# A gated feed-forward stage in seven block products instead of eight, joined on VectorE, and a new order in the openings of the conv phases

## What is computed

```python
def _L3_ffn_ref(x, U1, V1, U2, V2, b1, b2):   # HIDDEN 1024, INTER 2752, RANK 256
    P = jnp.einsum('bsh,hr->bsr', x, U1)
    H = jnp.einsum('bsr,rf->bsf', P, V1) + b1
    gate, up = (H[..., :INTER], H[..., INTER:])
    act = jax.nn.silu(gate) * up
    Z = jnp.einsum('bsi,ir->bsr', act, U2)
    out = jnp.einsum('bsr,rh->bsh', Z, V2) + b2
    return out
...
x = x + _L3_ffn_ref(_L3_cond_ref(x, cond_512, ...), L3_ffn_U1, L3_ffn_V1, L3_ffn_U2, L3_ffn_V2, L3_ffn_b1, L3_ffn_b2)
```

## Time and profile before

| | |
|---|---|
| median of 3 runs | 2100.54 us (2098.27 to 2106.67) |
| the profiled execution | 2105.4 us, its span 2103.2 us |
| mean granted clock of TensorE | 0.98 |
| busy in the span: TensorE, VectorE | 1970.7 us (94%), 1291.9 us (61%) |
| busy in the span: ScalarE, GpSimd | 961.5 us (46%), 368.6 us (18%) |
| the gated stage | from about 1688 us to the end |

### The profile page before, as it was taken

How to read it: one execution, slowest core, us unless ns; L and a number is a source line. 1 busy time by engine, 2 the same in 40 slices (tenths; PEclk the granted TensorE clock), 3 DMA queues, 4 the chain that set the end, 5 groups by cost and what they waited for, 6 DMA issues and landing times. The chain is left out here.

```text
span 2103.2 us, 32178 instructions
## 1 busy us (share of the span) xinstructions
PE 1970.7 (94%) x10213; PEld 1667.7 (79%) x10213; DVE 1291.9 (61%) x2326; ACT 961.5 (46%) x1547; POOL 368.6 (18%) x457
## 2 busy tenths in 40 slices
PE   4799968899999979998899999988999999999999
PEld 4688834799999868886788878877888878878886
DVE  6888888877767763327667676656555443344333
ACT  4488744555555421114344444424666544433442
POOL 4122212111111100002111111112121222222221
PEclk9899999999999999999999999999999999999999
DMA  7567547321121154444221112223333211142114
GB/s 189 175 194 198 175 166 244 94 67 60 60 89 61 51 188 150 136 133 147 72 71 60 51 55 64 66 65 120 101 100 110 82 54 45 52 140 88 49 45 164
DMA packets 118608, 222.30 MB, mean 106 GB/s; under 512 B 18336, under 2 KB 65184, under 8 KB 117792
## 3 DMA queue, kind: packets, MB, share of 16 engines
q1 hardware_dynamic: 102048, 212.36, 32.2%
q10 hardware_dynamic: 16512, 9.31, 1.6%
HBM read 159.04 MB, written 62.59 MB: 105 GB/s over the span
## 5 line engine op out<-in xcount | busy, mean ns | idle before, releaser
L2666 DVE SCALAR_TENSOR_TENSOR f_prod<-ps,b,f_gate 128x512 f32<-128x512 f32 (+1 forms) x88 | 66.0, 751 | 170.9 <-ACT f_gate L2606 170.9
L125 POOL TENSOR_TENSOR rows<-l_EY,ones 128x4 f32<-128x4 f32 x128 | 31.1, 243 | 740.0 <-ACT rows L1346 380.4
L2707 POOL TENSOR_TENSOR x_lo<-f_prod,x_hi 128x512 fp32r<-128x512 f32 (+1 forms) x88 | 105.0, 1193 | 288.2 <-ACT x_hi L2613 288.2
L2536 PE MATMUL ps<-pt_hi,v_hi 128*128 128x512 f32 (+1 forms) x352 | 138.0, 392 | 1.7 <-PEq L637 1.7
L2536 PE MATMUL ps<-pt_lo,v_hi 128*128 128x512 f32 (+1 forms) x352 | 137.8, 391 | 0.0
L2536 PE MATMUL ps<-pt_hi,v_lo 128*128 128x512 f32 (+1 forms) x352 | 137.2, 390 | 0.0
L2606 ACT ACTIVATE f_gate<-ps,b 128x512 f32<-128x512 f32 (+1 forms) x88 | 60.6, 689 | 157.8 <-PE ps L2536 157.7
L1085 PE MATMUL ps<-l_u_hi,l_g_hi 128*128 128x512 f32 x272 | 113.6, 418 | 5.7 <-DVE l_g_lo L1606 3.6
L1572 DVE SCALAR_TENSOR_TENSOR rows<-ps,dem3e,l_middle 128x512 f32<-128x512 f32 x60 | 45.1, 752 | 119.5 <-ACT l_middle L1315 97.4
L125 POOL TENSOR_TENSOR XE<-rows,ones 128x8 f32 (+1 forms) x96 | 21.1, 243 | 536.4 <-DVE rows L1782 260.8
L1085 PE MATMUL ps<-l_u_lo,l_g_hi 128*128 128x512 f32 x272 | 110.3, 406 | 0.0
(11 more groups left out here) (407 smaller groups left out, 5802.1 us busy)
## 6 DMA issues: line engine op xcount, KB each, us to landing
x<-rows SPq DMA_DIRECT2D x64, 512.0 KB, 2.9
xin<-x SPq DMA_DIRECT2D x96, 256.0 KB, 4.0
rows<-x SPq DMA_DIRECT2D x48, 512.0 KB, 4.1
out<-rows SPq DMA_DIRECT2D x32, 512.0 KB, 2.6
v<-in_ffn_v SPq DMA_DIRECT2D x84, 128.0 KB, 2.6
xin<-in_x SPq DMA_DIRECT2D x16, 512.0 KB, 5.8
xb<-in_x SPq DMA_DIRECT2D x16, 512.0 KB, 3.3
x<-xb SPq DMA_DIRECT2D x16, 512.0 KB, 2.6
```

The lines of the kernel that those rows point to most:

```text
L2536: mm = nc.tensor.matmul(ps[0:m, 2 * g + gu, :], v1sp[ws][:, s, r, gu, 0:m], pt[ms][:, r, cols], start=(k == 0), stop=(k == 5))
L2666: v.scalar_tensor_tensor(prod[0:m, g, :], ps[0:m, 2 * g + 1, :], b1[0:m, 1, bass.ds(2 * i + g, 1)], gate[0:m, g, :], ALU.add, ALU.mult).th ...
L2707: nc.gpsimd.tensor_tensor(asp[1][0:m, g, :], prod[0:m, g, :], asp[0][0:m, g, :].bitcast(F32), ALU.subtract).then_inc(al_ready, 1)
```

## The change

In the gated stage all blocks but n = 0 and n = 22 use a scheme of seven block products. The four outputs (gate and up, each for the two g) are a 2x2 product of weights (rank group r by gate or up) and tokens (r by g), which takes eight products of 128x128 by 128x512. The scheme takes seven, of mixed weights and mixed tokens, and adds products up afterwards:

- Weights: four mixes of the V1 block (additions and subtractions of 128x128, `mix_v1`), split like V1 itself (128x512, lines 2658 and 2800). One own quarter isn't used as such, so the own split has 384 columns.
- Tokens: at the start of each half `raw_tokens` adds high and low part again (128x2048), `mix_tokens` makes four mixes (128x512), and their high and low parts follow as 128x2048. The second half's stand between its first half's output additions.
- Products: seven of three matmuls each. Products 1 and 4 add up in bank 0, 2, 5 and 6 in bank 1, 3 and 7 in bank 2 or 3.
- Joins on VectorE (`join`, line 2814), 128x512 each, a bank plus an SBUF tile: `second` = bank 1 + `first`; `part` = bank 1 + `first`; `part` += bank 2 or 3; `first` += bank 1; `second` += bank 2 or 3. `first` is ScalarE's copy of bank 0 after product 1 (`read_first`, 2700). The gate for g = 0 is read out of bank 0, the gate for g = 1 out of `second`, up for the two out of `first` and `part`, all three in SBUF.
- V2 is split in two halves, in blocks 1 and 20, instead of at the start.
- ScalarE splits the U2 block n at the start of block n instead of at the end of block n-1, and copies bank 0 ahead of the high part of g = 1's product.

In the openings `edges_p` waits for the split low part of u instead of `g_summed` and writes banks 7 and 1; a group of four filling matmuls becomes one of two; ScalarE does `cross_g(0)` ahead of chunks that stood before it, and `split_h(0)` ahead of one; VectorE does `split_h(0)` ahead of a chunk; GpSimd's chunks wait for the low part of g.

```diff
             def edges_p():
                 pe.wait_ge(ue_ready, n)
-                pe.wait_ge(g_summed, g0 + 1)
+                pe.wait_ge(ul_ready, 2 * g0 + 2)
...
                     edges_p()
                     if layer > 0:
-                        K.turn_over(nc, ps, 7, 4)
+                        K.turn_over(nc, ps, 4, 2)
                     main(0)
...
+            if len(chunks) > 0:
+                pool.wait_ge(gl_ready, g0 + 1)
             for k in range(min(POOL_CHUNKS, len(chunks))):
                 chunk(k)
...
+                def seven(i, n, s, short, half=half):
...
+                    pe.wait_ge(w_lo, 2 * n + 1)
+                    pe.wait_ge(silu_ready, 2 * n - 1)
+                    product(0, m, own(1, 0), tokens(1, 0), True)
+                    if isinstance(n, int) and n == half * NIB + 1:
+                        pe.wait_ge(prod_ready, 2 * n)
+                        pe.wait_ge(mix_t_lo, used + half + 1)
+                    else:
+                        pe.wait_ge(joined, used + 5 * at - 1)
+                    product(1, m, mixed(2), mixed_tokens(0, 1), True)
+                    product(2 + s, m, mixed(0), mixed_tokens(1, 0), True)
+                    pe.wait_ge(first_ready, used + at + 1)
+                    product(0, m, own(0, 0), tokens(0, 0), False)
+                    pe.wait_ge(joined, used + 5 * at + 1)
+                    product(1, m, mixed(1), mixed_tokens(1, 1), False)
+                    project(i - 1, n - 1, 1 - s, 0, False)
+                    pe.wait_ge(joined, used + 5 * at + 2)
+                    product(1, m, own(0, 1), mixed_tokens(0, 0), False)
+                    pe.wait_ge(joined, used + 5 * at + 3)
+                    product(2 + s, m, mixed(3), tokens(0, 1), False)
+                    project(i - 1, n - 1, 1 - s, 1, False)
...
+            def read_first(n, m, half):
+                act.wait_ge(gu_done, products_before(n, half) + 1)
+                act.wait_ge(prod_ready, 2 * n - 1)
+                nc.scalar.activation(first[0:m, :], ps[0:m, 0, :], ACT.Copy).then_inc(first_ready, 1)
...
+            def join(n, half, k, out, src, bank, m):
+                product = (2, 5, 5, 6, 7)[k]
+                at = 5 * (n - half - 1)
+                dve.wait_ge(gu_done, products_before(n, half) + product)
+                if k == 0:
+                    dve.wait_ge(first_ready, used + n - half)
+                if k == 1:
+                    dve.wait_ge(prod_ready, 2 * n)
+                if k > 1:
+                    dve.wait_ge(joined, used + at + 2)
+                v.tensor_tensor(out[0:m, :], ps[0:m, bank, :], src[0:m, :], ALU.add).then_inc(joined, 1)
...
+                if is_whole(n):
+                    up = ps[0:m, 2 * g + 1, :]
+                else:
+                    dve.wait_ge(joined, used + 5 * (n - half - 1) + 4)
+                    up = (first, part)[g][0:m, :]
...
+                    join(n, half, 0, second, first, 1, m)
+                    split_u2(n, s, short)
+                    if not last and not is_whole(n + 1):
+                        mix_v1(n + 1, 1 - s, next_short, half)
+                    join(n, half, 1, part, first, 1, m)
+                    join(n, half, 2, part, part, 2 + s, m)
+                    if not last:
+                        split_v1(n + 1, 1 - s, next_short)
+                    join(n, half, 3, first, first, 1, m)
+                    multiply(i, n, 0, m, half)
+                    join(n, half, 4, second, second, 2 + s, m)
+                multiply(i, n, 1, m, half)
```

More of the change, by code:

```diff
@@ L1428, in first_pair @@
                 cross_g(1)
[L1429 to L1431 removed]
+                if layer == 0:
                     split_g(1)
                 split_h(0)
[L1434 to L1437 removed]
+                if layer > 0 and not fast:
+                    split_g(1)
                 some_chunks(len(chunks))
@@ L2468, in gated_ffn @@
         asp = [t[:, :, 0:HALF] for t in K.Xs]
+        part = sb("part", [P, HALF])
+        mix_w = sb("mix_w", [P, 4, P])
+        mix_wsp = [sb("mix_w_hi", [P, 2, 4, P], F32R), sb("mix_w_lo", [P, 2, 4, P], F32R)]
+        mix_t = K.c_raw[:, 0:2 * T].rearrange("p (r t) -> p r t", r=2)
+        mix_tsp = [t[:, 0:2 * T].rearrange("p (r t) -> p r t", r=2) for t in K.c_part]
+        first, second = K.xin[:, 0, :], K.xin[:, 1, :]
         zsp = [sb("z_hi", [P, 2, T], F32R), sb("z_lo", [P, 2, T], F32R)]
@@ L2479, in gated_ffn, with is_whole, products_before @@
         block = ctx.enter_context(nc.Block())
+        def is_whole(n):
+            return isinstance(n, int) and n % NIB == 0
+        def products_before(n, half):
+            return 7 * n - 5 * (half + (not is_whole(n)))
         def blocks(eng, half, body):
@@ L2539, in gate_up, with product @@
                     mm.then_inc(gu_done, 1)
-                def project(i, n, s, g, short):
-                    m = rows_of(short)
-                    pe.wait_ge(al_ready, 2 * n + g + 1)
-                    if g == 0:
-                        pe.wait_ge(w_lo, 2 * n + 2)
-                    start = isinstance(i, int) and i == 0
-                    if start and half == 1 and g == 0:
-                        pe.wait_ge(xo_ready, NT)
-                    for r in range(2):
+                def product(out, m, weights, moving, start):
+                    for k, (ws, ms) in enumerate(PASSES):
+                        mm = nc.tensor.matmul(ps[0:m, out, :], weights[ws], moving[ms],
+                                              start=(start and k == 0), stop=(k == 2), skip_group_check=True)
+                    mm.then_inc(gu_done, 1)
@@ new lines, in project @@
+                def project(i, n, s, g, short, ranks=(0, 1)):
+                    m = rows_of(short)
+                    start = isinstance(i, int) and i == 0
+                    if 0 in ranks:
+                        pe.wait_ge(al_ready, 2 * n + g + 1)
+                        if g == 0:
+                            pe.wait_ge(w_lo, 2 * n + 2)
+                        if start and half == 1 and g == 0:
+                            pe.wait_ge(xo_ready, NT)
+                    for r in ranks:
@@ L2588, in _, with split_v1 @@
         def _(act):
-            def split_v1(n, s, short):
+            def split_v1(n, s, short, half):
                 m = rows_of(short)
@@ L2620, in body @@
                 last = short and n == 2 * NIB - 1
-                silu(i, n, 0, m)
-                if not last:
-                    split_v1(n + 1, 1 - s, next_short)
-                act_hi(n, 0, m)
-                silu(i, n, 1, m)
-                act_hi(n, 1, m)
-                if not last:
-                    split_u2(n + 1, 1 - s, next_short)
+                after = half + (isinstance(i, int) and i == NIB - 1)
+                if is_whole(n):
+                    silu(i, n, 0, m, half)
+                    if n == 0:
+                        mix_tokens(0)
+                    else:
+                        split_u2(n, s, False)
+                    split_v1(n + 1, 1 - s, next_short, after)
+                else:
+                    split_u2(n, s, short)
+                    if not last:
+                        split_v1(n + 1, 1 - s, next_short, after)
+                    silu(i, n, 0, m, half)
+                act_hi(n, 0, m)
+                silu(i, n, 1, m, half)
+                if is_whole(n):
+                    act_hi(n, 1, m)
+                    if n > 0:
+                        mix_tokens(1)
+                if not short:
+                    read_first(n + 1, rows_of(next_short), half)
+                if not is_whole(n):
+                    act_hi(n, 1, m)
+                if isinstance(n, int) and n in (1, NIB - 2):
+                    split_v2(int(n > 1))
+            act.wait_ge(const_loaded, 32)
             for half in range(2):
-                blocks(act, half, body)
+                blocks(act, half, lambda i, n, s, first, short, half=half: body(i, n, s, short, half))
                 for g in range(2):
@@ new lines, in mix_tokens @@
+            def mix_tokens(half):
+                g0, g1 = slice(0, HALF), slice(HALF, T)
+                done = 5 * half
+                for k, (r, g, left, right) in enumerate((
+                        (1, g0, (1, g1), (1, g0)), (1, g1, (0, g1), (1, g1)),
+                        (0, g1, (0, g1), (1, g0)), (0, g0, (0, g0), (0, g1)))):
+                    dve.wait_ge(mix_t_ready, used + done + k + 1)
+                    v.tensor_tensor(mix_t[:, r, g], mix_t[:, left[0], left[1]], mix_t[:, right[0], right[1]],
+                                    ALU.subtract).then_inc(mix_t_ready, 1)
@@ L2660, in split_u2, with multiply @@
                                 ALU.subtract).then_inc(w_lo, 1)
-            def multiply(i, n, g, m):
+            def multiply(i, n, g, m, half):
                 dve.wait_ge(silu_ready, 2 * n + g + 1)
```

157 lines of the change are left out of this document (113 added, 44 removed).

## The result

The changed kernel took 2180.22 us (median of 4 runs, 2172.92 to 2187.27) against 2101.47 (4 runs): a ratio of 1.0377, 95% interval 1.0350 to 1.0405. A second set gave 2174.40 (5 runs), ratio 1.0348 (1.0308 to 1.0388). The forecast was 2162, range 2130 to 2190, slower with 0.90. The profiled execution took 2172.92 us, its span 2171.1.

What follows compares the result with a forecast made beforehand. TensorE's matmuls bound the gated stage before; VectorE's dependent chain would bound it after. Intervals +53.6, edges +6.1 + 3.4 + 0.7 + 3.0 - 4.4 + 4.5 and openings -5.5 gave +61.4, so 2162 us, range 2130 to 2190.

Steps and rivals of the forecast that it cites:

- The interval: Gated stage, block to block: VectorE's chain takes 9.62 us against 8.28 before, +53.6 us over 40 intervals.
- u_lo: VectorE's low part of U2 in each block: held by GpSimd's instruction, ending 2.12 us after the second multiply.
- Second product: VectorE's second multiply in each block: two SBUF operands, held by GpSimd, ending 0.61 us after it, at 9.62.
- TensorE stays the bound: Rival for the gated stage: VectorE's chain under 7.6 us, interval 7.58, time about 2080; chance 0.06.
- The edges: Gated stage outside steady intervals: start +6.1, V2 split +3.4, mixing +0.7, block 23's weights +3.0, first intervals -4.4, half ends +4.5.
- Start: Start of the gated stage: block 1 begins at 1699.8 against 1693.7 before, +6.1 us.
- end of the first half: Last projection of the half waits for VectorE, ScalarE and GpSimd: 2.25 us at each half's end, +4.5 for both.
- mixes of tokens and outputs: Second half's token mixing, placed between the first half's output additions: +0.7 us.
- the one on the clock: Rival for the gated stage: TensorE's stalls lower the clock, +4.6 us an interval, 2346 if throughout; chance 0.04.
- The split of V2: V2's split, moved in halves to blocks 1 and 20 behind the second multiply: 1.7 us each, +3.4.
- The openings: Openings of the four conv phases: edge product no longer waits for VectorE's sum; -5.5 us, between 0 and -14.
- No overlap of VectorE's instructions: Rival: each VectorE instruction starts only when the previous ends, 10.4 us a block, 2194; over 2190, this or register waits: 0.05.

Runs made afterwards that it cites:

- pool_short: Changed kernel with GpSimd's low part of the product cut from 512 to 16 columns a time: interval 8.63 us, gated stage 447.2 us.
- join4_early_pool_short: Changed kernel with join4 and second silu moved earlier and GpSimd's low part cut to 16 columns: 2099.86 us, ratio 0.9996 to before; interval 7.71.
- extra_add: Changed kernel with one more 128x512 VectorE addition and a wait in each of the 42 mixed blocks: interval 10.16 us, stage 512.4 us.
- filled: Changed kernel with unread filling matmuls in four of TensorE's pauses in the gated stage: stage 481.6 us, whole 2168.1 and 2168.3 us.
- after_again: The changed kernel unedited, run for a second trace: 2184.96 us, gated stage 488.1 us.
- join4_early: Changed kernel with join4 ahead of the first product on VectorE, second silu ahead of the first high part on ScalarE: 2139.13 us, ratio 1.0192 to before.

## Why the prediction came out as it did

**The interval: right, and its steps too.** Forecast 9.62, measured 9.58. u_lo: end at +2.12 forecast, +2.11 seen. Second product: 0.61 after GpSimd forecast, 0.55 seen, and 1.05 instead of 0.75 long. Wait for the silu 1.00. pool_short gave the price without holding that the prediction had named as a bound (8.7; measured 8.63), join4_early_pool_short came near the 7.58 of TensorE (7.71), and extra_add showed that one chain goes through VectorE. The sum of the intervals (with the first ones, the wait for block 23's weights and one split of V2) was 53.6 - 4.4 + 3.0 + 1.7 = 53.9, and the two stretches of 20 blocks grew by 26.88 + 27.25 = 54.1. Single terms in it were off: block 1's interval was 9.56 and not 7.6 (with its pause filled it was 7.80, so the half rate made the difference), and a gain came at block 24 instead (7.99).

**The rival "TensorE stays the bound": wrong, and shown why.** Its 6.57 us of VectorE work is a sum from start to start; where nothing is held (join4_early_pool_short) VectorE is busy 90.47 of 100 us at 7.71 a block, 6.98, so it was right to 0.4. The time from there to 9.58 is waits and holding.

**The edges: too small by 6.7.** Start 7.3 instead of 6.1; end of the first half 7.3 instead of 2.25 + 1.7; end of the second 2.6 instead of 2.25; mixes of tokens and outputs 2.5 instead of 0.7. The step that failed is the one on the clock: I asked only whether the half rate would hold throughout the stage and took the fp8 stage's 1.00 as the answer. (That row's 79% is a busy share; the busy share of the changed loop is 88.96, its share by count 79.6.) In the loop the answer was right (clock 1.00 at pauses of 0.3 to 0.7 us). At the edges the pauses are 1.5 to 6.0 us, and filled, which took most of the half rate away, has the terms nearly as forecast: start 6.2, end of the first half 4.3, of the second 1.5, mixes of tokens and outputs 1.4, the whole stage 66.4 above before, against the forecast 66.9. Single terms are still off by up to 0.8, and 1.5 us of half rate are in it behind block 2, so that it comes so close in sum is partly luck. The start's 7.3 holds 1.1 of block 0 at the half rate, which after_again doesn't have (6.2 there). The split of V2 was right behind block 1 (1.8) and too small behind block 20 (2.6 instead of 1.7).

**The openings: wrong.** I took -5.5, between 0 and -14. Measured was +1.2 (ratio 0.9990 to 1.0039, so -2 to +8). The sentence on GpSimd's subtractions had the mechanism, "they lie over other two-SBUF instructions", but I gave back only a part of the gain to it. In fact 9.3 us of waits became 14.0.

**No overlap of VectorE's instructions: fell.** In the changed kernel join0 starts at 1766.24, 0.08 before the product's end (1765.34 + 0.98), as in the earlier trace rows, and the round took 9.58 and not 10.4. The Trainium skill ("VectorE: DVE Perf Modes", section "The DRAIN you can't avoid") says that the next instruction doesn't start until the pipe is empty, and in the same paragraph that one that isn't held starts earlier. The prediction took up only the first sentence; join0 agrees with the second by its 0.08.

**The total**: 66.9 for the gated stage against 73.8, -5.5 for the openings against +1.2, 61.4 against 73 to 79. The two errors, 6.9 and 6.7, have the same sign and add up. What was measured lies 12 to 18 us above the 2162; that the range to 2190 still holds it is owed to its width, which was meant for the interval and not for these two. The profiled execution lies 7 us below its own set's median; layer 2's repeats (after_again) are the likely reason, which lie ahead of the stage that was changed.

## What to carry to other kernels

Before work is moved from the bound engine to an idle one, write its steps out as one loop: from an instruction back to itself in the next round, through every engine that it waits for. Here 6.57 us of instructions on an engine that was 39% busy made a round of 9.58. And where an instruction stands in the order decides more than its length: one swap (join4 ahead of the first product, and on ScalarE the silu that follows it) won 35 us of the 74. In the openings GpSimd's subtractions were laid over two-SBUF work in three places, and none made the kernel faster.

## What the runs showed of the hardware

- A VectorE instruction with two SBUF operands that starts while GpSimd's subtraction runs ends 0.28 (u_lo, 128x256, all 37 such) or 0.55 us (second product, 128x512, all 40) after it. Other sizes in the changed kernel and join4_early: 0.15 (128x128), 0.41 (128x384), 2.15 (128x2048). Alone these take 0.42, 0.75, 0.28, 0.55 and 2.29, so each ends 0.13 to 0.20 less than its own duration after GpSimd, as if nothing of it ran before. With a PSUM operand it isn't held (0.45 beside 2.07 for its neighbours). One that started ahead of GpSimd isn't held either (0.75, join4_early).
- TensorE's granted clock stays at 1.00 through a loop with pauses of 0.3 to 0.7 us in each block, 79.6% of the time in matmuls. After single pauses of 1.5 to 6.0 us at the edges, some seven matmuls follow 0.43 apart, but not after every one: a pause of 3.24 us in block 2 was followed by matmuls 0.23 apart, the same one (3.23) in filled by matmuls 0.43 apart.
- In both kernels a repeat of layer 2 takes 25.4 us, or 27.2 to 28.8 where TensorE pauses 1.8 us at line 1165. One execution of the changed kernel had none of the longer ones, another had six, and 12 us lay between the two.
